# A subtraction on GpSimd put behind a VectorE instruction, and VectorE's short instructions in another order

## The reference

```
q, k, v = split(x, 3, axis=1)                       # each 125 x 512
w = softmax(einsum('bct,bcs->bts', q*s, k*s))       # 512 x 512 per entry, s = 125**-0.25
h = einsum('bts,bcs->bct', w, v)                    # 125 x 512
h = h + attention(layernorm(h))    # 8 heads, 2 kv heads, rope, scores tanh-capped at 50, Wo
h = h + ffn(layernorm(h))
# ffn: softmax gate over 8 experts, top 2 by score plus bias, experts 512 -> 448 -> 512
#      with silu(x w1) * (x w3), plus a shared expert of the same form on every row
```

## Time and profile before

| | us |
|---|---|
| median of 3 runs | 6112.19 |
| lowest, highest | 6110.96, 6116.32 |
| the profiled execution's own time | 6103.52 |
| its span, first to last instruction | 6101.8 |

### The profile page before, as it was taken

One profiled execution on the slowest core, in us unless ns is written; L12 is line 12 of the kernel. 1 busy time (PEld: TensorE's weight loads), 2 busy tenths in 40 slices (PEclk: granted clock), 3 DMA queues, 4 the chain that ended last, 5 costly groups with the idle time before them and its releaser, 6 DMA issues. The chain is left out here.

```text
span 6101.8 us, 109407 instructions
## 1 busy us (share of the span) xinstructions
PE 5794.5 (95%) x32259; PEld 5032.2 (82%) x32259; DVE 4321.1 (71%) x9591; ACT 3413.1 (56%) x6260; POOL 2064.2 (34%) x1711
## 2 busy tenths in 40 slices
PE   5999999999999999999999999699999999999999
PEld 4777877777777777777777778599999999999998
DVE  3777777777777777777777777566767767766766
ACT  4555555555665556656566555355555555555554
POOL 1333333333333333333333333234333433443443
PEclk8999999999999999999999999899999999999999
DMA  2111111111111111111111111477777767777762
GB/s 71 43 42 46 46 43 42 42 44 46 44 42 43 45 46 44 42 43 46 45 44 42 42 45 38 120 187 182 188 186 185 184 183 187 187 183 187 188 161 83
DMA packets 363663, 565.45 MB, mean 93 GB/s; under 512 B 92898, under 2 KB 187106, under 8 KB 363492
## 3 DMA queue, kind: packets, MB, share of 16 engines
q1 hardware_dynamic: 294276, 433.22, 23.9%
q0 software_dynamic: 69344, 131.70, 10.7%
HBM read 438.14 MB, written 138.42 MB: 94 GB/s over the span
## 5 line engine op out<-in xcount | busy, mean ns | idle before, releaser
L1425 POOL DMA_INDIRECT out_dram<-res,goal x273 | 547.5, 2006 | 1062.2 <-DMA entries<-routed_entries 485.5
L944 POOL TENSOR_TENSOR vT_low<-vT_full,vT_high 128x500 fp32r<-128x500 f32 x128 | 162.8, 1272 | 1741.4 <-ACT vT_high L691 1741.4
L1175 PE MATMUL ps<-rT_hi,up_hi 128*128 128x384 f32 x2548 | 552.6, 338 | 1.6 <-DVE rT_lo L1335 1.6
L1175 PE MATMUL ps<-rT_lo,up_hi 128*128 128x384 f32 x2548 | 552.3, 338 | 0.0
L962 POOL DMA_INDIRECT routed_entries<-entry,slot x256 | 320.5, 1252 | 685.0 <-DVE slot L905 635.4
L1175 PE MATMUL ps<-rT_hi,up_lo 128*128 128x384 f32 x2548 | 552.1, 338 | 0.0
L624 ACT ACTIVATE e<-ps,negmax 128x512 f32<-128x512 f32 x512 | 350.1, 686 | 340.6 <-PE ps L437 296.4
L1265 ACT ACTIVATE uT_hi<-egb 128x384 fp32r<-128x384 f32 x364 | 191.4, 526 | 572.5 <-DVE egb L1354 561.9
L1175 PEld LDWEIGHTS ps<-rT_hi,up_hi 128*128 128x128 f32 x2548 | 458.3, 188 | 9.9 <-issue 2.0
L1175 PEld LDWEIGHTS ps<-rT_lo,up_hi 128*128 128x128 f32 x2548 | 456.4, 188 | 0.0
L1175 PEld LDWEIGHTS ps<-rT_hi,up_lo 128*128 128x128 f32 x2548 | 456.3, 188 | 0.0
(11 more groups left out here) (220 smaller groups left out, 15327.9 us busy)
## 6 DMA issues: line engine op xcount, KB each, us to landing
raw<-in_L_ffn_w SPq DMA_DIRECT2D x182, 768.0 KB, 5.1
X<-in_x SPq DMA_DIRECT2D x128, 750.0 KB
raw<-in_L_ffn_w SPq DMA_DIRECT2D x91, 896.0 KB
raw<-in_L_ffn_w SPq DMA_DIRECT2D x273, 128.0 KB, 5.1
normed_rows<-y SPq DMA_DIRECT2D x128, 250.0 KB
out_dram<-h SPq DMA_DIRECT2D x128, 250.0 KB
rows<-normed_rows,entries POOLq DMA_INDIRECT x273
out_dram<-res,goal POOLq DMA_INDIRECT x273
```

The lines of the kernel that those rows point to most:

```text
L1175: ins = nc.tensor.matmul(ps[:, bank, 0:GROUP], w[a][:, k, col:col + P], rT[b][:, k, :], start=(k == 0 and i == 0), stop=(k == KC - 1 and i ...
L1425: nc.gpsimd.indirect_dma_start(out, bass.IndirectOffsetOnAxis(ap=goal[group[1] % 2][:, i:i + 1], axis=0), res[i][:], None, bounds_check=la ...
```

## The change

GpSimd waits for `y_sb` of entry t-2 ahead of `cut_scores` for entry t+1, where both exist. On VectorE the expert choice is cut in two behind `max`: `xT_lo`, `rz` and the two `attn` halves now stand between `max` and `max_index`. And the low parts of `qkT` stand ahead of `h3`.

```
@@ VectorE @@
                         chosen(nc.vector.max(v8[0:C, :], met[0:C, :]))
+                    if has(1):
+                        dve.wait_ge(xT_hi.sem, xT_hi.at(a))
+                        lo_part(xT, 3).then_inc(xT_lo.sem, 1)
+                    if has(0):
+
+                        dve.wait_ge(e_sb.sem, e_sb.at(t))
+                        dve.wait_ge(e_norm.sem, e_norm.at(a))
+                        nc.vector.reciprocal(rz[:, :], total[:, :]).then_inc(rz_sb.sem, 1)
+                    if has(2):
+                        normalise(0)
+                        normalise(1)
+                    if has(3):
                         alone(dve)
                         chosen(nc.vector.max_index(i8[0:C, :], v8[0:C, :], met[0:C, :]))
...
                         nc.vector.tensor_tensor(m16[0:C, :], oh[0:C, 0, :], oh[0:C, 1, :],
                                                 ALU.add).then_inc(m16_sb.sem, 1)
-                    if has(1):
-                        dve.wait_ge(xT_hi.sem, xT_hi.at(a))
-                        lo_part(xT, 3).then_inc(xT_lo.sem, 1)
...
-                        normalise(0)
-                        normalise(1)
...
-                    if has(3):
-
-                        dve.wait_ge(dn_ps.sem, dn_ps.at(g))
-                        dve.wait_ge(h3_out.of(back(g, 2)), h3_out.at(back(g, 2)))
-                        nc.vector.tensor_tensor(h3[pg][0:C, :], ps[0:C, 6, :], h2[pg][0:C, :],
-                                                ALU.add).then_inc(h3_sb.sem, 1)
                     if has(1):
                         dve.wait_ge(qkT_hi.sem, qkT_hi.at(a))
...
                                                 ALU.subtract).then_inc(qkT_lo.sem, 1)
+                    if has(3):
+
+                        dve.wait_ge(dn_ps.sem, dn_ps.at(g))
+                        dve.wait_ge(h3_out.of(back(g, 2)), h3_out.at(back(g, 2)))
+                        nc.vector.tensor_tensor(h3[pg][0:C, :], ps[0:C, 6, :], h2[pg][0:C, :],
+                                                ALU.add).then_inc(h3_sb.sem, 1)
@@ GpSimd @@
                         rstd(f, ag2, ve2, rs2, ag2_sb, ve2_sb, rs2_sb, y_sb)
                     if has(-1):
+                        if has(2):
+                            pool.wait_ge(y_sb.sem, y_sb.at(f))
+                            alone(pool)
                         cut_scores(back(t, -1))
```

More of the change, by code:

```diff
@@ L799, in step @@
                         chosen(nc.vector.max(v8[0:C, :], met[0:C, :]))
[L800 to L808, removed]
                     if has(1):
@@ L819, in step @@
                         normalise(1)
+                    if has(3):
+                        alone(dve)
+                        chosen(nc.vector.max_index(i8[0:C, :], v8[0:C, :], met[0:C, :]))
+                        chosen(nc.vector.tensor_copy(i2[0:C, :], i8[0:C, 0:2]))
+                        for k in range(2):
+                            chosen(nc.vector.tensor_scalar(oh[0:C, k, :], iota8[0:C, :], i2[0:C, k:k + 1], None,
+                                                           ALU.is_equal))
+                        dve.wait_ge(rank_ps.sem, rank_ps.at(back(g, 1)))
+                        nc.vector.tensor_tensor(m16[0:C, :], oh[0:C, 0, :], oh[0:C, 1, :],
+                                                ALU.add).then_inc(m16_sb.sem, 1)
                     if has(2):
```

## The result

| | before | after |
|---|---|---|
| median us | 6111.57 (6102.52 to 6116.32, 4 runs) | 5853.22 (5852.18 to 5855.11, 4 runs) |
| profiled execution | 6103.52 | 5854.09 |
| span | 6101.8 | 5852.4 |

The changed kernel is faster: ratio 0.9579, 95% interval 0.9563 to 0.9596. That is 258 us by the medians and 249 us by the profiled executions; the forecast was 5930, a saving of 181 us, and the range ended at 5875. The direction was right, and so was the cause given for TensorE's two large waits; the size was not, and the new wait that the forecast took off does not appear.

The account below looks back on a forecast made before the run. TensorE was taken to bound the kernel, with small holes in the tower. Per step 0.92 + 0.81 - 0.38 + 0.1 = 1.45 us, over 125 steps 181 us, gave 5930 us; range 5875 to 5995.

Parts of the forecast that it names:

- two holes: TensorE's waits in each tower step for VectorE's y (0.92 us) and qkT_lo (0.81 us), together 1.73 us, forecast to come back.
- rival A: Routed entries on VectorE not held by qk_low, so no wait at xT_hi: 1.83 us a step saved, 5883 us; chance 0.25.
- part 3: xT_lo, rz and attn ahead of the expert indices on VectorE: 0.1 us a step alone, much more beside GpSimd's wait.
- part 1: GpSimd's qk_low waits for y_sb: y takes 0.55 us, 0.92 us a step back; about 0.8 without the indices moved.
- New wait: 0.38 us: TensorE's weight loads would wait 0.38 us a step for ScalarE's xT_hi, taken off the saving.
- slot's lead of 0.6 us: VectorE's slot would end only 0.6 us sooner, with the entries held by qk_low, while TensorE is 1.73 us ahead.
- The lap: Chain from slot through scatters, xn and xT_hi to TensorE and the next slot; forecast to make TensorE wait 0.38 us.
- the scaled e: TensorE's wait for ScalarE's scaled e, late because rz stood behind the expert indices; forecast to return 0.1 us a step.
- the clock: TensorE's clock falling to half level for 3.4 us a few times in the tower; worth some us, left out.

Follow-up runs that it names:

- part 1 without it: Only GpSimd's wait for y_sb ahead of cut_scores added to the kernel before, VectorE's order untouched: 5961.15 us, ratio 0.9756.
- part 3 alone: Only the four expert index instructions moved behind attn on VectorE in the kernel before: 6066.85 us, ratio 0.9928.

## Why the prediction was wrong in size

**Right.** y alone takes 0.55 us; TensorE's two holes at y and qkT_lo close; qkT_lo runs at full speed beside qk_low; the entries are held until qk_low ends (rival A's premise was false, though its time, 5883, was the nearest of all); part 3 is worth much more beside part 1 than alone (0.87 against 0.29 us a step; I had 0.1 for it alone, and 0.8 us a step for part 1 without it, which gave 29.32 - 28.25 = 1.07); the second stage keeps its length; qk_low's later end costs nobody anything. From y's start to slot's end I had 2131.85 - 2126.22 = 5.63 us, and it took 2132.04 - 2126.39 = 5.65. The hand-over to qk_low took 0.41 us and not 0.28, but the first junk ends with qk_low, where I had it start there.

**Wrong, the step that failed: "New wait: 0.38 us" at xT_hi.** I carried slot's lead of 0.6 us along the chain of the earlier trace rows and added 0.1. At least two links of that chain were themselves held by TensorE before, and so came sooner as TensorE did. In the earlier trace rows gb has "0.25 <-PE ps": from ga to gb it was 0.86 us there (2108.56 to 2109.42) and is 0.65 now (2110.18 to 2110.83). And xT_hi started at 2111.66 because TensorE's transposes of xn had just ended, a row that the prediction does not use:

```profile
2110.95 0.59 PE L412 MATMUL ps<-ident,xn 125*128 125x125 f32 x4
```

From e to xT_hi it was 2111.66 - 2110.81 = 0.85 us and is 2112.81 - 2112.14 = 0.67 now. From slot's end to xT_hi's end: 2112.25 - 2103.18 = 9.07 us before, 2113.39 - 2104.88 = 8.51 after. These are two steps of different kinds, since the steps differ in turn; over all steps from 200 to 3400 us the means are 9.15 and 8.65, so the chain is 0.50 us shorter, not 0.1. Of the 0.50, 0.19 lie between ga and gb and 0.13 between e and xT_hi; the rest lies before xn and behind gb, and what shortened it is not shown. And TensorE is less far ahead than I took: in the mean the two holes give 1.64 us, not 1.73 (below). Together that is more than the 0.38 of the forecast wait and leaves about the 0.06 to 0.10 us to spare that the experiments measure. The lap is real and is the next bound, at the link that the forecast named, but it stands about 0.1 us a step behind TensorE and not 0.38 ahead.

**Undersized: the scaled e.** I took 0.1 us a step; the weight loads' row gave 0.22, and part 3 alone confirms 0.20.

**Put at nothing: the clock.** The prediction named it and left it out. The kernel before has short stretches in which the granted clock is at its lower level, 1.2 GHz. One, by the view of stretches (TensorE alone):

```profile
2012.80:2016.20 3.40, 3.40 (x9) 0.50 0.32 76
```

The slots around it:

```profile
2013.82 0.17 DVE L905 CAST slot<-slotf 125x2 int32<-125x2 f32 x1
...
2044.56 0.17 DVE L905 CAST slot<-slotf 125x2 int32<-125x2 f32 x1
```

That step took 30.74 us, where others take 29.15 or 29.29 in turn. There are eight such stretches between 190 and 3500 us. Seven long steps fall into the 111 of the step length of 29.32; the other 104 have a mean of 29.23, so the clock costs 0.09 us a step, about 1.5 us for each stretch. In the changed kernel there is none in that part. Each stands just behind the two waits, about 1 us before a slot. But the two waits do not bring it about by themselves: with part 3 alone both are as long as before (75.7 and 72.7 us from 200 to 3400 us, 76.2 and 72.0 before), and the clock fell once instead of eight times:

```profile
3390.40:3393.80 3.40, 3.40 (x10) 0.50 0.31 77
```

Its four runs have a mean granted clock of 0.989 to 0.991, like the changed kernel's, and those of the kernel before 0.985 to 0.989. Part 3 alone takes away only the short wait for the scaled e; what sets the lower clock off is not shown.

**The sum again**, a step, from the starts of TensorE's matmuls in all steps from 200 to 3400 us. From the last blend to the transposes of y it was 1.16 and 1.03 us in turn and is 0.23: 0.86 in the mean. The 0.92 of the prediction came from a step of the first kind; this is one of the second:

```profile
2040.11 0.40 PE L454 MATMUL ps<-e_cut_hi,vT_low 128*125 128x512 f32 x1
2041.14 0.64 PE L412 MATMUL ps<-ident,y 125*128 125x125 f32 x4 [0.64 <-DVE y L870]
```

From the transposes to the next product it was 1.30 and is 0.52: 0.78, since my 0.49 was 0.03 too short. With the scaled e and the clock that is 0.86 + 0.78 + 0.20 + 0.09 = 1.93 us, measured 1.94. Against the forecast's 1.45: +0.38 for the wait that is not there, +0.10 for the scaled e, +0.09 for the clock, -0.09 for the two holes. In 125 steps 1.94 us is 243 of the 249 us by the spans; about 1 of the other 6 is the second stage, and the rest was not followed. The medians differ by 258, since the profiled execution of before was 8 us faster than its median and that of after was not. The scatter of the kernel before goes with its clock on the whole: over its runs beside the experiments, those with a mean granted clock of 0.989 took 6102 and 6104 us, those with 0.986 took 6114 to 6116, and the one with 0.985 took 6120. So more or fewer such stretches in a run fit the 8 us; only the profiled run shows them singly.

## What to carry to other kernels

Before a chain's length is carried over to a changed kernel, ask of every link what ended its wait: links that waited for the engine that gets faster come sooner along with it, and a chain measured while it was being held is only an upper bound. Where a difference of some tenths of a microsecond decides, read it from all steps and not from one, and look behind a listed wait whether a second one ends later. Two waits in a row on the busiest engine may be one cause seen twice: here a single semaphore on GpSimd removed both, and the reordering meant for the second added nothing, though without that semaphore it was worth 0.60 us a step. A third part that was worth 0.29 us a step alone was worth 0.87 beside the first.

## What the runs showed of the hardware

Two of VectorE's instructions that read and write SBUF, y and junk, stood still while GpSimd's subtraction ran, the second with only 8 columns: junk took 0.16 us alone and up to 1.14 us beside qk_low, y 2.51 us instead of 0.55. Instructions that read PSUM and one SBUF operand did not: h3 took 0.68 us beside it and alone. The Trainium skill, page "SBUF — State Buffer", section "SBUF: two separate sides", says that two SBUF inputs are enough for the exclusion where GpSimd reads SBUF; junk agrees. What I had not expected is how little it costs to let the long GpSimd instruction go second: it was on nobody's path, and a hand-over of 0.41 us closed two holes of TensorE.
